# Attention key masks as matmuls on 32 rows of the array, three side by side, for both tiles of a head at once

## What is computed

```python
sim = jnp.einsum('bhid,bjd->bhij', q, k)
sim = sim + bias
sim = jnp.where(causal_mask, neg, sim)
mask_p = jnp.pad(mask, ((0, 0), (1, 0)), constant_values=True)
sim = jnp.where(mask_p[:, None, None, :], sim, neg)
attn = jax.nn.softmax(sim, axis=-1)
out = jnp.einsum('bhij,bjd->bhid', attn, v)
```

## Time and profile before

| | us |
|---|---|
| median of 3 runs | 3011.5 (3011.39 to 3014.64) |
| the profiled execution | 3008.76 |
| its span, first to last instruction | 3007.0 |
| first attention core | 139 to 643 |
| second attention core | 1517 to about 2022 |

### The profile page before, as it was taken

How to read it: one execution, slowest core, us unless ns; L and a number is a source line. 1 busy time by engine, 2 the same in 40 slices (tenths; PEclk the granted TensorE clock), 3 DMA queues, 4 the chain that set the end, 5 groups by cost and what they waited for, 6 DMA issues and landing times. The chain is left out here.

```text
span 3007.0 us, 55507 instructions
## 1 busy us (share of the span) xinstructions
PE 2486.6 (83%) x16024; PEld 2025.3 (67%) x16024; DVE 1575.9 (52%) x4371; ACT 1325.8 (44%) x3147; POOL 972.3 (32%) x1298
## 2 busy tenths in 40 slices
PE   5799999988797853985789999998599998773895
PEld 3477777767686752973467777777477786772784
DVE  3366666644214345226767666654588885526111
ACT  2365666753222431323456666674344442242231
POOL 0143444321204555534333233322333330545002
PEclk9999999999797975997989999999799998995997
DMA  8122222211574363511022222210200001254684
GB/s 272 32 74 77 70 85 74 72 40 59 206 269 116 109 204 116 175 62 52 21 87 71 64 87 71 84 43 16 81 1 1 0 0 53 73 162 164 238 307 157
DMA packets 150859, 296.58 MB, mean 99 GB/s; under 512 B 25158, under 2 KB 110407, under 8 KB 144561
## 3 DMA queue, kind: packets, MB, share of 16 engines
q1 hardware_dynamic: 138416, 262.92, 26.0%
q0 software_dynamic: 12288, 31.83, 3.5%
HBM read 240.25 MB, written 64.56 MB: 101 GB/s over the span
## 5 line engine op out<-in xcount | busy, mean ns | idle before, releaser
L799 DVE CUSTOM_DVE_ANT_0 prob_l<-ps_l,bias_l,nsn 128x1024 f32<-128x1024 f32 (+3 forms) x256 | 276.7, 1081 | 107.6 <-DVEq L798 60.6
L799 DVE CUSTOM_DVE_ANT_0 cur_sb<-ps_h,bias_s,nsn 128x128 f32<-128x128 f32 (+3 forms) x256 | 139.7, 546 | 237.7 <-DVEq L798 237.4
L727 PE MATMUL ps_l<-khi,stage 128*128 128x512 f32 (+3 forms) x512 | 257.8, 503 | 0.0
L874 ACT ACTIVATE prob_l<-prob_l,nmax 128x1024 f32<-128x1024 f32 (+3 forms) x256 | 252.1, 985 | 2.2 <-DVE nmax L799 1.7
L733 PE MATMUL ps_pt<-ident_sb,prob_l 128*128 128x128 f32 x1664 | 236.4, 277 | 6.0 <-ACT cur_sb L858 2.1
L858 ACT ACTIVATE cur_sb<-ps_pt 128x128 f32<-128x128 f32 (+3 forms) x256 | 110.7, 433 | 264.3 <-PE ps_pt L733 264.3
L692 POOL TENSOR_TENSOR stage<-qo,stage 64x256 fp32r<-64x256 f32 x256 | 199.7, 780 | 47.8 <-POOLq L691 47.8
L733 PEld LDWEIGHTS ps_pt<-ident_sb,prob_l 128*128 128x128 f32 x1664 | 185.9, 141 | 36.5 <-ACT cur_sb L858 15.4
L284 PE MATMUL ps_q<-wf,xnT 128*128 128x512 f32 (+1 forms) x384 | 149.9, 544 | 63.4 <-ACT xnT L321 52.0
L683 POOL COPY nsn<-nsn 128x4 f32 (+1 forms) x128 | 26.2, 204 | 527.0 <-DVE diff L816 378.6
L2273 POOL TENSOR_TENSOR ss<-simx,sim 128x4096 f32<-128x4096 f32 x16 | 113.4, 7085 | 238.2 <-DVE simx L2422 238.2
(11 more groups left out here) (338 smaller groups left out, 6166.9 us busy)
## 6 DMA issues: line engine op xcount, KB each, us to landing
mlp_ws<-in_L_ffn_experts_dram SPq DMA_DIRECT2D x39, 2052.0 KB, 7.5
xs<-slot_rows SPq DMA_DIRECT2D x156, 128.0 KB, 2.1
slot_outputs<-ys SPq DMA_DIRECT2D x156, 128.0 KB, 1.9
slot_rows<-zero_sb SPq DMA_DIRECT2D x1, 16384.0 KB, 52.3
bias_l<-in_fside_16xSxS_dram SPq DMA_DIRECT2D x16, 512.0 KB, 3.4
mlp_w<-in_L_ffn_experts_dram SPq DMA_DIRECT2D x8, 1024.0 KB, 7.9
bias_by_partition<-bias_table SPq DMA_DIRECT2D x16, 512.0 KB, 4.1
bias_l<-bias_by_partition SPq DMA_DIRECT2D x16, 512.0 KB, 3.3
```

What stands on the lines that cost most here:

```text
L727: ins = pe.matmul(out, stage[:, b, s, x.h % 2, x.h // 2, :], att[part][:, b * S + lo:b * S + hi], start=False, stop=part == "klo", skip_gr ...
L799: dve.tensor_tensor_reduce(out=spans(x, prob), in0=scored(x), in1=spans(x, bias), scale=-1.0, scalar=nsn[:, b, s, h:h + 1], op0=ALU.add, o ...
L874: act.activation(prob[x.s][:, x.h, 0:x.W], prob[x.s][:, x.h, 0:x.W], ACT.Exp, bias=nmax[:, x.b, x.s, x.h:x.h + 1], scale=-1.0, accum_out=r ...
```

## The change

In `core_phase`, the mask matmuls of both tiles of a head are taken out of the slots' own sequence and issued together, at the start of the long slot: one for each half of the long tile and one for the short tile. Each contracts over 32 partitions in place of 128 (rows 0 to 31, 32 to 63, 64 to 95); as weights serves `lead16`, zero but for rows 0, 32, 64 and 96, which are one, so that one row of `km` reaches all outputs. The three write three different banks. With them moves the wait for the negation of the previous head's short tile, from the short slot to the long slot, where it stands after the two long masks. The `khi` and `klo` matmuls keep their places. In `setup`, POOL's copy of the identity to bf16 goes, and VectorE fills `lead16` with five memsets.

```diff
@@ setup
-            pool_eng.wait_ge(made, 1)
-            pool_eng.tensor_copy(c["ident16"][:], c["ident"][:]).then_inc(made, 1)
+
+        @block.vector
+        def _(dve):
+            dve.memset(c["lead16"][:], 0.0).then_inc(led, 1)
+            dve.wait_ge(led, 1)
+            for row in range(0, P, 32):
+                dve.memset(c["lead16"][row:row + 1], 1.0).then_inc(led, 1)
@@ core_phase, Slot
+                self.partner = None if w % 2 else Slot(p, g, w + 1)
@@ core_phase, tensor
+            def target(x, j, lo, hi):
+                return ps_h[:, 0:hi] if x.s else ps_l[:, x.h % 2, j * BANK:j * BANK + hi - lo]
+
+            def masks(*slots):
+                row = 0
+                for x in slots:
+                    pe.wait_ge(dve_s[x.s].sem, dve_s[x.s].after("neg", x.n - (1 if x.s else 2)))
+                    for j, (lo, hi) in enumerate(halves(x)):
+                        pe.matmul(target(x, j, lo, hi), c["lead16"][row:row + 32], att["km"][row:row + 32, x.b, lo:hi],
+                                  start=True, stop=False, skip_group_check=True)
+                        row += 32
+
             def scores(x):
                 s, W, b = x.s, x.W, x.b
                 if x.h == 0:
                     pe.wait_ge(gp_s[s].sem, gp_s[s].after("lo1", x.pair))
 
-                pe.wait_ge(dve_s[s].sem, dve_s[s].after("neg", x.n - (1 if s else 2)))
+                if not s:
+                    masks(x, x.partner)
                 for j, (lo, hi) in enumerate(halves(x)):
-                    out = ps_h[:, 0:W] if s else ps_l[:, x.h % 2, j * BANK:j * BANK + hi - lo]
-                    pe.matmul(out, c["ident16"][:], att["km"][:, b, lo:hi], start=True, stop=False, skip_group_check=True)
+                    out = target(x, j, lo, hi)
                     for part in ("khi", "klo"):
                         ins = pe.matmul(out, stage[:, b, s, x.h % 2, x.h // 2, :], att[part][:, b * S + lo:b * S + hi],
                                         start=False, stop=part == "klo", skip_group_check=True)
```

More of the change, by code:

```diff
@@ L165, in setup @@
         made = ph.sem()
+        led = ph.sem()
         block = ph.stack.enter_context(nc.Block())
@@ L2533, in constants @@
     return {"x": sb("x_sb", [P, NT, D]), "cur": sb("cur_sb", [P, NT, D]), "ident": sb("ident_sb", [P, P]),
-            "ident16": sb("ident16", [P, P], BF16), "ones": sb("ones_sb", [P, P]), "eps": sb("eps_sb", [P, 2]), "zero": sb("zero_sb", [P, D])}
+            "lead16": sb("lead16", [P, P], BF16), "ones": sb("ones_sb", [P, P]), "eps": sb("eps_sb", [P, 2]), "zero": sb("zero_sb", [P, D])}
 N_PHASE_SEMS = 40
```

## The result

The changed kernel takes 3251.8 us (median of 4 runs, 3245.9 to 3254.5) against 3011.4: 1.0795 of the time before, 95% interval 1.078 to 1.0809. It is slower by 240 us. Forecast were 141 us and 3153; the range ended at 3210.

A forecast was written before the change was run, and what follows sets the result against it. The attention cores were taken as bound by PE's instruction stream, then by the loop the moved wait closes: 3008.8 + 141 = 3149.8 us, 3153 against the median, with setup and row switching at 0; range 3095 to 3210.

The forecast's parts named there:

- PE is ahead of the short negation, so the moved wait bites: At the long slot, PE arrives 1.1 to 1.4 us before the previous short negation ends, in three of four pairs.
- The loop, +141 us: Attention cores: long scores, long negation and short negation form a closed loop; 2.2 us per four-head quad, 64 quads.
- R: Loop time from a short negation's end to the next long negation's start: 1.43, 1.36, 1.31, 1.24 us at p = 0 to 3.
- the sum: Predicted time per quad (four heads of one batch, eight alternating long and short slots): 18.0, 17.8, 18.0, 18.0 us.
- VectorE's part with the totals: Slots 2 and 3 of a quad: start of long negation to end of short one, totals between, 2.43 us.
- The part of slots 0 and 1: VectorE's time there from start of the long negation to end of the short one, 1.56 us.
- The price of 32 rows, taken at 0, other end 41 us: Switching PE to 32 rows and back at the masks: taken as 0; upper bound 0.16 us for each of 256 pairs.
- costly switching: Rival: going to 32 rows and back costs over 0.2 us a pair on top, 3205 us and more; chance 0.06.
- The clock: Rival: PE's idling in the cores drops the clock to 1.2 GHz, +640 us, 3650 us; chance 0.02.
- That is the whole gain there can be: Three masks side by side take the time of one: 0.29 us saved per long and short pair, 256 pairs, 73 us.
- All other phases unchanged: Sign of being right: phases outside the two attention cores keep their times.

The follow-up runs named there:

- e3: Kernel before the change plus one wait: at the long slot PE also waits for the previous head's short negation; masks on 128 rows in their own slots. 3247.4 us.
- e1: Changed kernel with its order and moved wait kept, but every mask matmul contracts over all 128 partitions instead of 32. 3175.4 us.
- e8: Changed kernel with only the short mask put back on 128 rows; the two long masks stay on 32. 3175.9 us.
- e6: Kernel before the change without any mask matmul, so the key mask is left out of the scores; serves as a bound only. 2966.2 us.
- e4: Changed kernel regrouped: short mask issued at the short slot with the next head's long masks, on 32 rows side by side, no moved wait. 3011.5 us.
- e5: Same as e4, but all masks use the same rows 0 to 31, so they cannot run side by side. 3077.8 us.
- e10: Same grouping as e4, no moved wait, but every mask over 128 rows. 2999.2 us.

## Why the prediction was wrong

The direction, the place and the mechanism of the loop were right; the size was not, because the price of going to 32 rows and back was put at nothing. By the steps of the forecast:

- **PE is ahead of the short negation, so the moved wait bites.** Right: PE waited in three of four pairs. e3 shows it with nothing else changed.
- **The loop, +141 us.** e1 holds it without the rest: +164. R came out to 0.05 us. The quads of e1 take 18.2, 18.3, 18.1 and 18.4 us, where the sum has 18.0, 17.8, 18.0 and 18.0: 18 of the 23 us. At p=0 and 1, from the long scores of slot 4 to those of slot 6, where the values stand, e1 takes 6.84 us; the sum has 6.6 (with the 0.2 for long masks that no wait hides) and 6.65, some 7 us in all. At p=1, too, PE comes to the long masks of slot 6 only when the short negation is ending, which the sum allowed for at p=0 alone. PE and VectorE in e1:

```profile
390.50 1.05 PE L751 MATMUL ps_pt<-ident_sb,prob_l 128*128 128x128 f32 x7
391.39 0.54 PE L731 MATMUL ps_l<-km,lead 128*128 128x448 bf16 x2
391.77 0.27 PE L731 MATMUL ps_h<-km,lead 128*128 128x256 bf16 x1
```

```profile
390.96 0.48 DVE L817 CUSTOM_DVE_ANT_0 cur_sb<-ps_h,bias_s,nsn 128x256 f32<-128x256 f32 x1 [3.59 <-DVEq L816]
```

  VectorE's part with the totals was 2.44 to 2.68 us on average, where I took the shortest, 2.43: some 6 us. The part of slots 0 and 1 was 1.74 at p=3 for 1.56: 3 us. The rest wasn't followed up.
- **The price of 32 rows, taken at 0, other end 41 us.** This is the step that failed. R in the changed kernel is longer than in e1 by 0.14, 0.19, 0.19, 0.20 us at p = 0 to 3 (medians ahead of slots 0 and 2), mean 0.18, and 256 x 0.18 = 46 us. e8 puts it at the short mask's way out. The upper bound, 0.16, was nearly the value; I took the other end because a change between bf16 and fp32 weights costs little, and that was no neighbour of a change of rows. The weight load of khi starts 0.26 us behind the 32-row mask and together with the 128-row one (549.99 in the changed kernel, 544.05 in e8). The Trainium skill's page "TensorEngine Tiling (Array Packing)" (Key Properties) says that a change of tiling mode drains the engine; these rows agree with it, and it had spoken for the upper end. The rival "costly switching", over 0.2 us a pair and 3205 or more, had 0.06. The time lies in its region, but not by its price alone, which came to 0.18: the loop and the clock brought the rest.
- **The clock.** I had asked whether it would fall for good and given that 0.02. It fell in 22 short dips, 30 us; why there and not in e1 is open. The row that I relied on, 2175 to 2417 at 0.99 with PE busy 92%, held waits too (ten in the list of waits, up to 2.0 us) and kept its clock, as e1 did; it could not show the dips. The rival's own number had a slip: 10 us a quad over the forecast's 18 belong on 3153, which makes 3793, not 3650.
- **The sum.** 141 + 23 + 46 + 30 = 240. The 23 are what e1 measured over the forecast; the 46 and 30 are estimates from rows, and together they are the 76 us between e1 and the changed kernel, and between e8 and it. The range took its risks one at a time, and they came together. They are not independent: e8 changes the short mask alone and takes away the price and most of the dips.
- **"That is the whole gain there can be", 73 us.** Too high: without any mask the kernel wins only 46 (e6). The Trainium skill's page "TensorE: Matmul & The Clock Gate" (Measured speedup vs the span model) has 3.07x for four tiles side by side; no run here shows that factor. The traces agree that the masks start together (e4 against e5), but at this place three of 384 columns win 0.14 us of 0.32, with the way out taken off, and the way in takes 0.11 more (e4 against e10).
- **All other phases unchanged.** Nearly: some 10 of the 244 us between the profiled executions lie outside the cores and were not followed up.

## What to carry to other kernels

Before an instruction is issued earlier, ask for each of its waits when it is met today, and compare the moment with that at which the engine would now stand there; if the engine runs ahead of that moment because a buffer is doubled, moving the wait forward undoes the doubling (e3: one wait, 236 us). The same grouping can often be had by moving the other member: here the long masks to the earlier short slot, where the existing wait covers both (e4, e10). Going from 128 rows to 32 cost about 0.1 us on the way in (e4, e10) and 0.14 to 0.20 on the way out (changed kernel, e8), so a group must save more than that; three masks of some 400 columns side by side did not make the kernel faster than the same three on 128 rows (e4 against e10).

## What the runs showed of the hardware

- Matmuls on three different groups of 32 rows and into three banks start within 0.01 us of each other; on the same 32 rows they follow at 0.17 us, about their 384 columns at 2.4 GHz (e4, e5).
- Behind the start of a mask on 32 rows khi starts 0.26 us after it, behind one on 128 rows 0.04 (changed kernel, e8), so that short mask to last klo grows from 0.71 to 0.88 us. Ahead of it, transposes to mask grow by 0.11 us (e4, e10). The same three masks one after another take 0.87 us to klo on 32 rows and 0.68 on 128 (e5, e10).
- In the changed kernel the clock fell 22 times for a few microseconds to 1.2 GHz, each time behind a wait of PE of 1.3 to 1.8 us; e1, with as much waiting, PE busy 86% as well and masks on 128 rows, had no such fall.
